# Four experts at a time by a broadcast product on VectorE, their sum on GpSimd, and a new order of steps: a two-layer transformer kernel

## What is computed

```python
x = x + _L0_attn_ref(xn, ...) + _L0_ffn_ref(xn, ...)   # xn = layernorm(x)
# in _L0_ffn_ref:
gate = jax.nn.softmax(x @ W_gate + b_gate, axis=-1)
top_g, top_i = jax.lax.top_k(gate, TOP_K)
combine = jnp.sum(jax.nn.one_hot(top_i, E) * top_g[..., None], axis=2)
expert_out = jnp.einsum('bsd,edf->bsef', x, W_experts) + b_experts
moe_out = jnp.einsum('bsef,bse->bsf', expert_out, combine)
return attn_out + moe_out
```

## Time and profile before

| | |
|---|---|
| Median of 3 runs | 2048.47 us (2047.59 to 2049.12) |
| The profiled execution | 2050.03 us, span 2048.2 us |
| ScalarE busy | 1875.9 us (92%) |
| VectorE busy | 1790.3 us (87%) |
| TensorE busy | 1625.1 us (79%) |
| GpSimd busy | 1062.5 us (52%) |
| Mean granted TensorE clock | 0.924 of full speed |

### The profile page before, as it was taken

The page is one execution under the profiler, slowest core; times in us unless marked ns, Lnnn a source line. Parts: engine busy times, 40 slices in busy tenths (PEclk is TensorE's granted clock), DMA queues, the critical chain, the costliest instruction groups (busy, mean ns, idle before and its releaser), DMA issues.

```text
span 2048.2 us, 39684 instructions
## 1 busy us (share of the span) xinstructions
PE 1625.1 (79%) x12405; PEld 796.0 (39%) x12405; DVE 1790.3 (87%) x4071; ACT 1875.9 (92%) x2144; POOL 1062.5 (52%) x448
## 2 busy tenths in 40 slices
PE   2678788888888888888888888888888888887865
PEld 1233444433444443344444334444433444443433
DVE  5778989999998999999899999989999998998844
ACT  2399999999999999999999999999999999999991
POOL 1455555456555545655554565555456555545520
PEclk9979999999999999999999999999999999999875
DMA  1000000000000000000000000000000000000000
GB/s 41 4 4 1 6 6 0 5 6 5 6 5 6 0 5 6 5 6 5 6 0 5 6 5 6 5 6 0 5 6 5 6 5 6 0 5 7 4 4 6
DMA packets 21059, 11.21 MB, mean 5 GB/s; under 512 B 1431, under 2 KB 20953, under 8 KB 20956
## 3 DMA queue, kind: packets, MB, share of 16 engines
q1 hardware_dynamic: 20956, 10.20, 1.7%
HBM read 6.00 MB, written 4.19 MB: 5 GB/s over the span
## 4 chain that ended last, share of the span: by engine, by line
ACT 40%; DVE 23%; issue 22%; PE 13%; POOL 1%; DVEq 1%; ACTq 1%; SPq 0%; DMA 0%; POOLq 0%
ACT curve L532 21%; ACT root L532 7%; ACT prob L532 3%; PE psM L1167 3%; DVE nmax L858 3%; DVE curve L848 3%; PE psM L1004 2%; ACT L563 2%; ACT L636 1%; PE psV L1199 1%; DVE h L421 1%; ACT hqT L532 1%; POOL qk L514 1%; PE psM L1151 1%; DVE hqT L417 1%
## 5 line engine op out<-in xcount | busy, mean ns | idle before, releaser
L532 ACT ACTIVATE curve<-curve 128x2048 f32<-128x2048 f32 x384 | 717.7, 1902 | 4.8 <-POOL curve L503 3.4
L500 POOL TENSOR_TENSOR root<-curve 128x2048 f32<-128x2048 f32 x128 | 460.1, 3600 | 426.1 <-DVE curve L852 425.9
L532 ACT ACTIVATE root<-root 128x2048 f32<-128x2048 f32 x256 | 484.4, 1905 | 8.1 <-POOL root L500 7.8
L503 POOL TENSOR_TENSOR curve<-curve,root 128x2048 f32<-128x2048 f32 x64 | 348.8, 5452 | 93.3 <-ACT root L532 93.3
L852 DVE TENSOR_SCALAR curve<-psS 128x1024 f32<-128x1024 f32 x256 | 306.0, 1216 | 25.3 <-PE psS L1035 19.1
L858 DVE TENSOR_REDUCE nmax<-psS 128x4 f32<-128x1024 f32 x256 | 308.8, 1214 | 7.2 <-PE psS L1044 6.9
L1199 PE MATMUL psV<-prob,vf 128*32 128x256 f32 x2048 | 270.8, 425 | 3.9 <-ACT prob L532 0.6
L532 ACT ACTIVATE prob<-psS 128x1024 f32<-128x1024 f32 x256 | 261.3, 1021 | 11.8 <-PE psS L1065 11.0
L1199 PE MATMUL psV<-curve,vc 128*32 128x256 f32 x2048 | 225.4, 408 | 40.0 <-ACT curve L532 36.3
L520 POOL TENSOR_TENSOR stk<-qk,stk 128x512 f16<-128x512 f32 x128 | 168.4, 1325 | 155.3 <-ACT stk L532 155.3
L848 DVE TENSOR_TENSOR curve<-curve,root 128x2048 f32<-128x2048 f32 x64 | 177.7, 2777 | 5.6 <-ACT root L532 5.6
(11 more groups left out here) (190 smaller groups left out, 2856.9 us busy)
## 6 DMA issues: line engine op xcount, KB each, us to landing
xt<-in_L_attn_x SPq DMA_DIRECT2D x32, 128.0 KB, 2.2
out<-yo SPq DMA_DIRECT2D x32, 128.0 KB, 1.8
we<-in_L_ffn_W_experts SPq DMA_DIRECT2D x1, 512.0 KB
curve<-in_L_attn_w_qkv SPq DMA_DIRECT2D x1, 192.0 KB
curve<-in_L_ffn_w_down SPq DMA_DIRECT2D x1, 176.0 KB
curve<-in_L_ffn_w_gate SPq DMA_DIRECT2D x2, 64.0 KB
...
```

Source lines behind the costliest of these rows:

```text
L500: nc.gpsimd.tensor_tensor(root[:, two], curve[:, p, two], curve[:, p, two], ALU.mult).then_inc(s_sq, 1)
L503: nc.gpsimd.tensor_tensor(curve[:, p, two], curve[:, p, two], root[:, two], ALU.mult).then_inc(s_half[0], 1)
L532: return nc.scalar.activation(out, in_, func, **kw)
```

## The change

It does two things. The weighting of the experts: VectorE multiplies a whole bank of four experts, 512 columns, by the four weights of each token, broadcast over the 128 channels, into a new buffer `scaled`; two such products per stage take the place of eight products-and-adds. GpSimd then adds the experts in pairs, the pairs, and the sum to `acc`, three instructions per stage. A bank is free again after the product. And the order of the steps is written anew; twelve steps also change their lag. Among them `c` 0 and `choose` 5 go from 1 to 0; `sq` 0 and `m` 4 from 0 to 1; `pvf` 7 from -1 to 0; `s1e`, `rs1` and `p1T` from -1 to -2; `quanth` 0 to 3 from -2 to -1.

In the loop, the order that follows from the list around `wexp` 3 is, on ScalarE: before, `wexp` 3, `ln` 0, `ln` 1, `oC`, `xnT`, `maxT`, `proj` 0, `ln` 2, `e` 0, `proj` 1, `norm`, `ocT`, `e` 1; after, `wexp` 3, `maxT`, `xnT`, `oC`, `e` 0, `o1`, `ln` 1, `proj` 0, `e` 1, `proj` 1. On TensorE: before, `pvw` 6, 7, `xnT`, `maxT`, `c` 6, 7, `proj` 0, `finc`, `e` 0, `proj` 1, `ocT`, `e` 1; after, `maxT`, `xnT`, `c` 5, `pvw` 6, 7, `e` 0, `o1`, `c` 6, `proj` 0, `pvf` 0, `c` 7, `e` 1, `proj` 1. GpSimd's order after: `experts` 0, `sq` 1, 2, 3, `fadd`, `experts` 1, `stack` 0, 1, `unit`, `mul` 0, `stack` 2, `mul` 2, `stack` 3, `sq` 0, `residual`.

```diff
 SCHEDULE = [
-    ("table", 0, -1), ("wln", 0, -1), ("c", 1, 0), ("sq", 0, 0), ("fadd", 0, -1), ("pvf", 7, -1), ("oF", 0, -1),
...
+    ("table", 0, -1), ("choose", 5, 0), ("wln", 0, -1), ("wln", 1, -1), ("c", 0, 0), ("oF", 0, -1), ("c", 1, 0),
+    ("wexp", 0, -1), ("s1e", 0, -2), ("quanth", 4, -2), ("experts", 0, 0), ("wexp", 1, -1), ("m", 5, 0), ("c", 2, 0),
+    ("pvw", 0, -1), ("wln", 2, -1), ("wln", 3, -1), ("p1T", 0, -2), ("sq", 1, 0), ("c", 3, 0), ("m", 6, 0),
+    ("pvw", 1, -1), ("sq", 2, 0), ("quanth", 5, -2), ("wexp", 2, -1), ("sq", 3, 0), ("ln0", 0, 1), ("fadd", 0, -1),
+    ("c", 4, 0), ("pvw", 2, -1), ("pvw", 3, -1), ("m", 7, 0), ("ln", 0, 0), ("experts", 1, 0), ("pvw", 4, -1),
+    ("wexp", 3, -1), ("rstd0", 0, 1), ("pvw", 5, -1), ("maxT", 0, 0), ("xnT", 0, 1), ("quanth", 6, -2), ("oC", 0, -1),
+    ("c", 5, 0), ("rs1", 0, -2), ("quanth", 7, -2), ("pvw", 6, -1), ("pvw", 7, -1), ("e", 0, 0), ("o1", 0, -2),
+    ("ln", 1, 0), ("c", 6, 0), ("proj", 0, 1), ("pvf", 0, 0), ("c", 7, 0), ("stack", 0, 1), ("quanth", 8, -2),
+    ("e", 1, 0), ("proj", 1, 1), ("finc", 0, -1), ("ln", 2, 0), ("norm", 0, 1), ("finf", 0, -1), ("e", 2, 0),
...
+        scaled = sb("scaled", [P, NT, 4, D])
...
-        s_ep, s_moe = sem("experts_in_psum", 4), sem("experts_added", 16)
+        s_ep, s_scaled = sem("experts_in_psum", 4), sem("experts_scaled", 4)
+        s_pair, s_four, s_moe = sem("expert_pairs_added", 2), sem("four_experts_added", 2), sem("experts_added", 2)
...
-            READ[("experts", j, 0)], READ[("experts", j, 1)] = (s_moe, 8 * j + 7), (s_moe, 8 * j + 8)
+            READ[("experts", j, 0)], READ[("experts", j, 1)] = (s_scaled, 2 * j + 1), (s_scaled, 2 * j + 2)
...
+                if stage == "experts":
+
+                    pool.wait_ge(s_scaled, due(s_scaled, b, 2 * arg + 2))
+                    nc.gpsimd.tensor_tensor(scaled[:, :, 0:2, :], scaled[:, :, 0:2, :], scaled[:, :, 2:4, :], ALU.add).then_inc(s_pair, 1)
+                    pool.wait_ge(s_pair, due(s_pair, b, arg + 1))
+                    nc.gpsimd.tensor_tensor(scaled[:, :, 0, :], scaled[:, :, 0, :], scaled[:, :, 1, :], ALU.add).then_inc(s_four, 1)
+                    pool.wait_ge(s_four, due(s_four, b, arg + 1))
+                    pool.wait_ge(s_acc0, due(s_acc0, b))
+                    if arg > 0:
+                        pool.wait_ge(s_moe, due(s_moe, b, arg))
+                    nc.gpsimd.tensor_tensor(acc[:, p, :, :], acc[:, p, :, :], scaled[:, :, 0, :], ALU.add).then_inc(s_moe, 1)
...
-                        dve.wait_ge(s_moe, due(s_moe, b - 2))
+                        dve.wait_ge(s_scaled, due(s_scaled, b - 2))
...
                 if stage == "experts":
-                    dve.wait_ge(s_acc0, due(s_acc0, b))
                     dve.wait_ge(s_gate, due(s_gate, b))
-                    for n in range(8):
-                        e, j = 4 * arg + n // NT, n % NT
+                    dve.wait_ge(s_moe, due(s_moe, b, arg))
+                    for j in range(NT):
                         bank, k = misc_bank(stage, arg, j)
-                        if n < NT:
-                            dve.wait_ge(s_ep, due(s_ep, b, NT * arg + j + 1))
-                        if 8 * arg + n >= NT:
-                            dve.wait_ge(s_moe, due(s_moe, b, 8 * arg + n + 1 - NT))
-                        nc.vector.scalar_tensor_tensor(acc[:, p, j, :], bank[:, (e % 4) * D:(e % 4 + 1) * D],
-                                                       comb[:, p, j, e:e + 1], acc[:, p, j, :], ALU.mult,
-                                                       ALU.add).then_inc(s_moe, 1)
+                        dve.wait_ge(s_ep, due(s_ep, b, NT * arg + j + 1))
+                        nc.vector.tensor_tensor(scaled[:, j, :, :], bank[:, :].rearrange("p (e f) -> p e f", f=D),
+                                                bc(comb[:, p, j, 4 * arg:4 * arg + 4], 2, D), ALU.mult).then_inc(s_scaled, 1)
```

34 lines of the change are left out of this document (13 added, 21 removed).

## The result

| | before | after |
|---|---|---|
| Median | 2048.11 us (2047.59 to 2049.12, 4 runs) | 2285.05 us (2278.22 to 2286.73, 4 runs) |
| Ratio, with its 95% interval | | 1.115 (1.1126 to 1.1174): slower |
| Span of the profiled execution | 2048.2 us | 2282.0 us |
| ScalarE busy | 1875.9 us | 1875.4 us |
| VectorE busy | 1790.3 us | 1894.0 us |

The change costs 237 us, where 31 were forecast. The direction was right, the size and its main cause were not.

The account below looks back on a forecast made before the run. It took ScalarE to set the pace, idle 2.8% of the time. New waits of +1.15 us a step times 31 (+36) and the tail (-5) gave +31, a median of 2079.5 us; range 2062 to 2098, over all cases 2030 to 2098.

Parts of the forecast that it names:

- ScalarE sets the pace, and only waits can cost: In the loop: ScalarE has 58.1 us of unchanged work and 1.7 us of idle time a step.
- A hold behind a square: Rival: GpSimd's squares hold VectorE's quantise steps up to 3.6 us; 2.7 us a step, 2163 us; chance 0.08.
- can each hold up a quantise step: Six added GpSimd instructions against VectorE: each a hold of at most 1.1 us, counted 0, up to 0.3 a step in range.
- Under 1 us of reserve: Before `maxT`, in the hold rival: row maxima held up by a square come late, with under 1 us to spare.
- the whole forecast of 1.15: Loop sum a step: +1.3 us passage, -0.37 old waits gone, +0.2 other places; +36 us over 31 steps.
- The narrow passage: From `wexp` 3 to `e` 1: TensorE's way 6.5 us, ScalarE's 5.17, so `e` 1 is 1.3 us late every step.
- The other places: `e` 2 behind `finf`, `p1` behind a lone `pvf` 5, half-angle products behind one another: 0.2 us a step (0 to 0.6).
- Product and adds: VectorE product 0.68 us; GpSimd adds 1.08, 0.72, 0.72 us per stage; VectorE busy down some 50 us, GpSimd's up some 160.
- The adds cost nothing: GpSimd's queue: 5.0 us of adds a step cost nothing while squares come two to three microseconds ahead of their logarithms.
- The tail: After the last table load: -5 us (-2 to -7), leaving about 60 to 63 us.
- The ramp: At the front, before the loop is steady: about as long in both orders, 0, within 3 us.

Follow-up runs that it names:

- q5_moved: The kernel after with one VectorE step, `quanth` 5, moved from behind `m` 6 to behind `maxT` and `xnT`: 2135.2 us, 1.0368 of the kernel before.
- order_only_residual_first: The kernel before with the new step order, its old products and no adds, and `residual` moved ahead of the first square: 2302.01 us, 1.1243 of the kernel before.
- q5_moved_filled: q5_moved with 16 transposes of the identity issued by TensorE before it waits for the row maxima: 2116.78 us, 1.0326 of the kernel before.

## Why the prediction was wrong, point by point

- **ScalarE sets the pace, and only waits can cost.** Right: its busy time is the same within 0.5 us, and all that was lost is its idle time.
- **A hold behind a square, nothing in the sum, at most 0.3 us a step in the range, a rival with 0.08.** This is the step that failed. The rival named the mechanism and, as one of three places, this one ("`quanth` 5 near the second square"); its price of 2.7 us was low as well, 4.8 by q5_moved. Its sign came true: ahead of `maxT` VectorE is the releaser of ScalarE's longest wait, 3.5 us, behind a step of 3.8 us. It was dismissed with "the steps are placed right behind the operation that releases the square". That looked at the release of the square alone. For `sq` 1 the release is not what lets it start: GpSimd is busy with `sq` 0, `residual` and the three adds until 1084.01 and starts it 0.16 us before VectorE gets to its step. Between two queues whose work is ready, the order of arrival has to be computed, and it wasn't. Nor do the adds decide it: order_only_residual_first has none, and a hold of its own in the same place.
- **The Trainium skill** (SBUF — State Buffer, section "SBUF: two separate sides") calls the lock exclusive. The held 16-column instruction, still 3.4 us long, agrees. I had read from it that the added instructions "can each hold up a quantise step" and priced the adds, when the dangerous instructions were the squares, three times as long and there all the time.
- **"Under 1 us of reserve" before `maxT`.** This is the second term that the sum had at nothing. There is no reserve: with `quanth` 5 away `mT` still waits 1.5 us a step, more than the whole forecast of 1.15. In the old order the reserve was larger: a hold of 2.1 us cost 0.5.
- **The narrow passage, 1.3 us late.** The size was right: in q5_moved_filled, at full clock, `oC` waits 0.36 us and `e` 1 another 0.90, together 1.26; in iteration 1 of the kernel after, which has no `o1` (0.78 us of TensorE), they wait 0.27 and 0.20. In part the agreement is luck: the forecast has `pvw` 6 released by `wexp` 3, but in q5_moved_filled `wexp` 3 is over at 1137.05 and `pvw` 6 starts at 1139.04, behind the late transposes; the 0.90 at `e` 1 is the chain as it was laid out. It couldn't be cured by moving `e` 1 alone. And it is 1.3 of the 7.9 us; most of the slowdown came from what the sum left out.
- **The other places, 0.2 (0 to 0.6).** Too small: the sigmoid's wait grew from 0.82 to 1.26 us a step and `p1`'s copy waits 0.5 (q5_moved), about 1.0 together. `p1` behind a lone `pvf` had been named.
- **The clock was left out.** The forecast took TensorE's durations from places where it had its full clock. TensorE stood longer and more often, and its mean fell from 0.924 to 0.796. Around the transposes of the row maxima that is 0.6 us a step by q5_moved_filled; what it costs at the end of the step wasn't separated.
- **Product and adds.** 684 ns for 680 forecast, 1273, 731 and 729 for 1080, 720 and 720. "The adds cost nothing" holds in a good place only (0.998, against 1.017). VectorE's busy time was to fall by 50 us and rose by 104, of which `quanth` 5 alone is 98 (from 18.2 in the kernel before to 116.2): a held instruction counts as busy. The rest are shorter holds that the new order brought elsewhere, as of the cast L821 (908 ns for 180) and the product L829 (1091 for 517). GpSimd's busy time rose by 270 us where 160 were forecast, 107 of it in the subtraction of `stack` (L522, 2152 ns mean for 1325): behind a half-angle product of VectorE (1124.49 to 1127.22) it takes 3.21 us, from 1125.03, where the unheld one takes 1.15. None of these was in the sum either, and no run moves them.
- **The tail, -5 us.** 57.6 us after the last table load, where 60 to 63 were forecast: right in sign, 2.4 us below the range. The ramp became 2.7 us shorter, within the 3 allowed.

What stays open: why `mT` is late in q5_moved by 1.5 us although VectorE has less to do than before (I read it as too much packed ahead of `maxT` in its queue, as the trace lays it out, but no run shows that it can be cured there), what the shorter holds of VectorE and GpSimd cost, and how the clock at the end of the step shares in the waits there. What lets TensorE's clock fall after one idle piece and not after another of the same length stays open too.
